# Four residual stages on one core: the node table projected from x itself, three steps behind the attention

## The chip, the core and the metric

The kernel runs on one core of a Trainium2 chip. The metric is device time in microseconds (us), the median of several runs of the whole program; a profiled execution of the same program is taken apart from them. TensorE is called PE in the rows, its weight load PEld, VectorE DVE, ScalarE ACT, GpSimd POOL, SyncE SP.

## What is computed

x holds 128 graphs of 128 nodes with 128 features. Four residual stages follow one another (layer norms in between): a graph attention with a given adjacency (GNN 0), a switch layer that sends each of 16,384 tokens to one of 8 experts (FFN 0), a second graph attention (GNN 1), and a layer whose gate is itself an attention over 524,288 random edges plus one loop per node, with 4 experts of which the top 2 are mixed (FFN 1). The change sits at the joint of the third and the fourth:

```python
x = x + gnn0(layernorm(x), adj, ...)
x = x + ffn0(layernorm(x), ...)
x = x + gnn1(layernorm(x), adj, ...)
x = x + ffn1(layernorm(x), edge_index, ...)

def ffn1(x, ...):
    h = x.reshape(M, 128) @ W_gat
    a_src, a_dst = (h * att_src).sum(-1), (h * att_dst).sum(-1)
    e = leaky_relu(a_src[src] + a_dst[dst])
    alpha = segment_softmax(e, dst)
    agg = segment_sum(h[src] * alpha, dst)
    ...
```

The layer norm of a row is (x - mean) times rstd, rstd = 1 / sqrt(var + eps). Of each node the edges need 24 numbers: 16 columns of h and 4 + 4 attention terms. They form the node table, 16,384 rows of 24.

## The kernel before

The program is two blocks with a barrier between them. **Block 1** (function front) does GNN 0, the routing, the first experts, the sort of the edges' keys and GNN 1, and writes the node table to DRAM. **Block 2** (edges_and_experts1) gathers table rows by edge and runs the last layer.

GNN 1 and all that stands beside it is one software loop over groups of 4 graphs, 32 groups. In step n each engine runs its part of several groups: TensorE turns the probabilities of group n (L221), makes the scores of n+2 (L228, L233, L237), turns the features of n+3 (L245), multiplies probabilities and values of n (L252), and makes the values of n+3 (L264). ACT copies what TensorE turned (L177, L192), makes the leaky branch of the scores (L181), normalises group n+4 (L90) and takes the exponentials of n+2 (L204). DVE divides by the sums and adds to x (L271, L279), takes the maximum of scores and leaky branch and its row maximum (L287, L289), adds the bias to the values of n+3 (L296) and takes the statistics of the finished group (L98). For n up to 16 DVE also adds an expert result to a later group and takes its statistics (combine, L756 and L98); these are called early steps, those from 17 on late ones.

Two more jobs are woven into the same loop. One is the **search**: POOL fetches eight blocks of 64 sorted keys with eight indirect DMAs (L1158) into one of four buffers, DVE compares them with the wanted keys (L818) and counts (L821). There are 32 searches; 25 stand in the loop, in steps n >= 0 whose n mod 4 isn't 3. POOL may begin fetch n only when search n - 4 is counted. The other is the **projection of the node table** (class Projection, tag gat). It follows the attention with a lag of 12 steps: ACT normalises a finished group (L90), TensorE turns it (L378) into bank 1, ACT copies it (L367), TensorE multiplies it with the 24-column weight (L384) into bank 3, and DVE keeps the result in the table in SBUF (L389). The four norms that it needs, of 8 groups each, are made in the loop (L116 to L136, root on ACT at L128). The twelve steps of lag run on behind the loop, with seven searches left beside them or behind them. Where a quarter of the table is kept, SP writes it to DRAM (L905).

In a step each engine follows its program's order, and semaphores say when. Where the projection stands in that order is written out by hand: on TensorE behind L264,

```python
for n in range(-3, GROUPS + LAG):
    att1.pe_step(pe, n, n % 4)
    gat.pe_step(pe, n - LAG, n % 4)
```

and on ACT behind the exponentials, on DVE behind the statistics, the combine and the norms.

Block 2's POOL loop has 31 turns. A turn issues 16 indirect DMAs for one part of the edges (gather(0), L1518), 16 for another (gather(1)), and then two that fetch windows of edge rows for DVE (L1524). Between them POOL takes from SP that the rows gathered before are written to the edge table (rows_out), and from DVE that the window buffer is free (win_free). SP writes the second part of a turn only when DVE has seen the turn's windows (win_seen). DVE scores a window (from L1391 on) and mixes the experts' outputs (L1480). One more pair of windows follows the loop.

Of the kernel before, what the change touches and what calls it, by code (L numbers as in the profile page):

```python
# [14 lines left out]
P = 128  # L15
GRAPHS = NODES = FEAT = 128
PER = 4
# [333 lines left out]


class Projection:
    def __init__(self, sem, tag, x, rstd, shift, ident, weight, cols, into, view, banks, lo=0, turned_in=(0, 1), put_in=(2, 3)):
        self.feat, self.featT = view(lo, 2, PER, FEAT), view(lo + 1024, 2, PER, NODES)
        self.b_featT, self.b_out = ([banks[:, k, :].rearrange("p (v i) -> p v i", v=PER) for k in pair] for pair in (turned_in, put_in))
        self.ahead = len(set(turned_in))
        self.normed, self.turned, self.featT_s, self.projected, self.kept = (
            sem(f"{tag}_{n}") for n in ("normed", "turned", "featT", "projected", "kept"))
        self.x, self.rstd, self.shift, self.ident, self.weight, self.cols, self.into = x, rstd, shift, ident, weight, cols, into  # L360

    def act_step(self, act, n, u):
            a, f = n + 1, n + 2
            if live(a):
                act.wait_ge(self.turned, a + 1)
                ge(act, self.projected, a - 1)
                act.activation(self.featT[:, (u + 1) % 2, :, :], self.b_featT[(u + 1) % 2][:, :, :], ACT.Copy).then_inc(self.featT_s, 1)  # L367
            if live(f):
                ge(act, self.turned, f - 1)
                normalise(act, self.feat[:, u % 2, :, :], self.x, self.rstd, self.shift, f).then_inc(self.normed, 1)  # L370

    def pe_step(self, pe, n, u):
            a = n + 1
            if live(a):
                pe.wait_ge(self.normed, a + 1)
                ge(pe, self.featT_s, a - self.ahead + 1)
                for v in range(PER):
                    last = pe.transpose(self.b_featT[(u + 1) % 2][:, v, :], self.feat[:, (u + 1) % 2, v, :], self.ident)  # L378
                last.then_inc(self.turned, 1)
            if live(n):  # L380
                pe.wait_ge(self.featT_s, n + 1)
                ge(pe, self.kept, n - self.ahead + 1)
                for v in range(PER):
                    last = pe.matmul(self.b_out[u % 2][:, v, 0:self.cols], self.featT[:, u % 2, v, :], self.weight, start=True, stop=True)  # L384
                last.then_inc(self.projected, 1)

    def dve(self, dve, n):
        dve.wait_ge(self.projected, n + 1)
        dve.tensor_scalar(self.into[:, n * PER:(n + 1) * PER, :], self.b_out[n % 2][:, :, 0:self.cols], 1.0, None, ALU.mult).then_inc(self.kept, 1)  # L389


def front(nc, sem, a, x, x_in, stats, scratch, rstd, shift, masked, tab, W, fills, ident, ones, upto, row_id, wanted, counted, found,
# [4 lines left out]
    with ExitStack() as ctx:  # L397
# [74 lines left out]
        gat = Projection(sem, "gat", x, rstd, shift, ident, gat_w[:, :], TAB, tab, view, banks, 4112, (1, 1), (3, 3))  # L472
# [53 lines left out]
        fetched = view(10256, FETCHED, SEARCH, FAN)  # L526
# [30 lines left out]
        def _(dve):  # L557
# [245 lines left out]
            while joined < CHUNK:  # L803
                combine(joined)
                joined += 1
            dve.wait_ge(got_stats, CHUNK)
            gnn1_norms[0].dve_before_root(dve)
            gnn1_norms[0].dve_behind_root(dve)
# [4 lines left out]
            def search():  # L813
                n = searched[0]
                searched[0] += 1
                cols = slice(n * SEARCH, (n + 1) * SEARCH)
                dve.wait_ge(fetched_s[n % FETCHED], 16 * SEARCH * (n // FETCHED + 1))
                dve.tensor_tensor(before[:, :, :], fetched[:, n % FETCHED, :, :],  # L818
                                  wanted[:, cols].unsqueeze(2).to_broadcast([P, SEARCH, FAN]), ALU.is_lt).then_inc(compared, 1)
# [36 lines left out]
            gat_norms[-1].dve_behind_root(dve)  # L856
            for n in range(GROUPS + 1 - LAG, GROUPS):
                gat.dve(dve, n)
                if n % 4 == 3 and searched[0] < SEARCHES // SEARCH:
                    search()  # L860
# [5 lines left out]
        def _(sp):  # L866
# [34 lines left out]
            table_v = table_dram.rearrange("(b i) c -> i b c", i=NODES)  # L901
            for c in range(GROUPS // CHUNK):
                cols = slice(c * CHUNK * PER, (c + 1) * CHUNK * PER)
                sp.wait_ge(gat.kept, (c + 1) * CHUNK)
# [4 lines left out]
        def _(pe):  # L909
# [93 lines left out]
                pe.matmul(to, by[:, :], held_v[:, :, 1], start=False, stop=True).then_inc(summed, 1)  # L1003
            pe.wait_ge(ranked_s, 1)
            pe.wait_ge(gat_made, 2)
            for n in range(-3, GROUPS + LAG):
                att1.pe_step(pe, n, n % 4)
                gat.pe_step(pe, n - LAG, n % 4)

        @block.scalar  # L1010
        def _(act):
# [86 lines left out]
            for n in range(-4, GROUPS + LAG):  # L1098
# [4 lines left out]
                if n > CHUNK and n % CHUNK == 1 and n // CHUNK <= len(gat_norms):  # L1103
                    gat_norms[n // CHUNK - 1].act_root(act)
                    act.wait_ge(gat_norms[n // CHUNK - 1].done, n // CHUNK)
                gat.act_step(act, n - LAG, n % 4)

        @block.gpsimd
        def _(pool):
# [44 lines left out]
            for n in range(SEARCHES // SEARCH):  # L1154
                ge(pool, looked, n - FETCHED + 1)
                for c in range(SEARCH):
                    q = n * SEARCH + c
                    pool.indirect_dma_start(fetched[:, n % FETCHED, c, :], None, keys_dram,  # L1158
                                            bass.IndirectOffsetOnAxis(row_ids[:, q:q + 1], 0)).then_inc(fetched_s[n % FETCHED], 16)


def edges_and_experts1(nc, sem, a, x, rstd, shift, node, found, counted, source_ids, row_id, table_dram, edges_dram, out, ident, ones):
# [8 lines left out]
    with ExitStack() as ctx:  # L1171
# [330 lines left out]
        def _(pool):  # L1502
# [11 lines left out]

            def gather(u):
                take(pool, ids_in[u], 16)
                for c in range(PART_TILES):
# [320 lines left out]
```

## Time and profile before

| | us |
|---|---|
| median of 3 runs | 3116.43 (3116.08 to 3119.05) |
| the profiled execution's own time, its span | 3601.8 |
| TensorE busy | 1935.1 (54%) |
| DVE busy | 2257.8 (63%) |
| ACT busy | 1215.1 (34%) |
| POOL busy | 1857.5 (52%) |

The profiled execution took 485.4 us longer than the median of the runs. It is described by its span alone. The second attention loop lies between about 1284 and 1723 us of that span, block 2's loop between 1881 and 3523.

In a timeline row the columns are: start, duration, engine, line of the program, operation, what it writes and reads, the number of merged instructions, and in brackets the idle time of the engine just before, with what ended it. In a row of groups the two times behind the bar are the busy time and the mean of one in ns, and then the idle time before them, by releaser. In a row of stretches each engine has its busy time with its count of instructions; PEclk is the clock that TensorE was granted, as a part of 2.4 GHz.

### The profile page before, as it was taken

Reading aid. Unit: us, or ns where it says so; the run is one execution under the profiler, and the core shown is the slowest. Engines: PE = TensorE matmul, PEld = TensorE weight load, DVE = VectorE, ACT = ScalarE, POOL = GpSimd, SP = SyncE. Lnnn points to the kernel's source line nnn. Section 1 sums busy time; section 2 is a strip of 40 time slices with the busy share of each in tenths; the row PEclk is TensorE's granted clock in tenths of the full one; section 3 lists DMA queues with packets and bytes.
Section 4 is the critical chain, followed back from the end, with each engine's and each line's share of the span. In section 5 each row is a group of like instructions: output and inputs, shape, how many; then the busy total and the mean of one; then the engine's idle time right before and its main releaser. Section 6 shows DMA issues by size and latency. Waiting matters only on the chain. (4 is left out here: it accounts for less than half of the span.)

```text
span 3601.8 us, 31245 instructions
## 1 busy us (share of the span) xinstructions
PE 1935.1 (54%) x8829; PEld 1316.8 (37%) x8829; DVE 2257.8 (63%) x4422; ACT 1215.1 (34%) x2447; POOL 1857.5 (52%) x1723
## 2 busy tenths in 40 slices
PE   1776642387878645567432455454544444454555
PEld 1555542255655434456311222232222222222223
DVE  8999886989999965554223454454553444544547
ACT  2676754244444323455311122122212122121222
POOL 5400248554544444445575656655655656656561
PEclk9998865699999867777555676676776677767768
DMA  5792001011111121101111111111111111111111
GB/s 198 250 391 84 16 23 39 24 40 37 46 44 41 36 60 40 56 20 23 42 27 23 32 33 32 32 28 38 32 33 32 32 28 31 38 28 32 37 29 30
DMA packets 170130, 192.35 MB, mean 53 GB/s; under 512 B 59241, under 2 KB 126096, under 8 KB 169008
## 3 DMA queue, kind: packets, MB, share of 16 engines
q1 hardware_dynamic: 107616, 118.69, 9.9%
q0 software_dynamic: 57088, 62.48, 8.4%
q10 hardware_dynamic: 5328, 9.97, 0.7%
q8 instruction: 49, 0.80, 0.1%
q14 instruction: 49, 0.40, 0.0%
HBM read 91.70 MB, written 105.25 MB: 55 GB/s over the span
## 5 line engine op out<-in xcount | busy, mean ns | idle before, releaser
L1518 POOL DMA_INDIRECT edge_rows<-node_table,edge_ids x1024 | 1006.5, 983 | 646.2 <-POOLq L1243 345.9
L1646 PE MATMUL x_b_hid<-x_featT,x_w 128*128 128x512 f32 x512 | 362.3, 854 | 281.4 <-PEq L1243 93.5
L1146 POOL DMA_INDIRECT token_results<-arena,token_of x160 | 251.1, 1569 | 294.3 <-ACT arena L1082 216.9
L583 DVE TENSOR_TENSOR sort_ping<-sort_pong 128x1024 f32<-128x1024 f32 (+1 forms) x232 | 395.1, 1744 | 11.3 <-issue 3.8
L1158 POOL DMA_INDIRECT arena<-keys,row_ids x256 | 249.3, 974 | 288.6 <-DVE counts L821 181.0
L583 DVE TENSOR_TENSOR sort_pong<-sort_ping 128x1024 f32<-128x1024 f32 (+1 forms) x230 | 389.9, 1736 | 8.7 <-ACT sort_ping L1016 3.7
L1139 POOL DMA_INDIRECT slots<-arena,send x128 | 177.8, 1389 | 371.9 <-ACT arena L1038 336.9
L1640 PE MATMUL x_b_featT<-ident,x_feat 128*128 128x128 f32 x128 | 34.8, 428 | 581.0 <-issue 385.3
L1653 PEld LDWEIGHTS x_b_res<-x_w,x_hid 128*128 128x128 f32 x2048 | 276.1, 216 | 152.1 <-issue 152.1
L1653 PE MATMUL x_b_res<-x_w,x_hid 128*128 128x128 f32 x2048 | 303.9, 307 | 39.8 <-issue 39.8
L1646 PEld LDWEIGHTS x_b_hid<-x_featT,x_w 128*128 128x128 f32 x512 | 118.9, 262 | 500.2 <-issue 300.9
L1600 ACT ACTIVATE x_hid<-x_b_hid,x_b 128x512 f32<-128x512 f32 x256 | 174.8, 687 | 294.9 <-DMA keys<-sort_pong 129.3
L90 ACT ACTIVATE arena<-x,shift,rstd 128x128 f32<-128x128 f32 x512 | 210.1, 486 | 98.8 <-DMA slots<-arena,send 87.5
L1640 PEld LDWEIGHTS x_b_featT<-ident,x_feat 128*128 128x128 f32 x128 | 22.9, 217 | 587.7 <-issue 587.7
L1607 ACT ACTIVATE w_taken<-w_taken 128x16 f32<-128x16 f32 x32 | 6.9, 216 | 586.5 <-ACTq L1243 357.3
L252 PE MATMUL banks<-arena 128*128 128x129 f32 x512 | 96.4, 347 | 183.3 <-DVE x L279 94.3
L1480 DVE SCALAR_TENSOR_TENSOR x_weighed<-x_b_res,gates,x_weighed 128x128 f32<-128x128 f32 x256 | 72.1, 344 | 193.9 <-DMA adjacent<-in_adj_dram 158.6
L1650 PE MATMUL x_b_res<-x_b,ones 1*128 1x512 f32 x256 | 162.9, 718 | 30.8 <-PEq L1243 27.0
L977 PEld LDWEIGHTS banks<-arena 128*128 128x128 f32 x1280 | 145.9, 192 | 30.3 <-issue 30.3
L252 PEld LDWEIGHTS banks<-arena 128*128 128x128 f32 x512 | 83.9, 248 | 194.1 <-issue 180.0
L977 PE MATMUL banks<-arena 128*128 128x128 f32 x1280 | 153.5, 278 | 0.0
L968 PE MATMUL banks<-arena 128*128 128x512 f32 x320 | 148.5, 608 | 1.8 <-issue 1.8
(346 smaller groups left out, 4059.0 us busy)
## 6 DMA issues: line engine op xcount, KB each, us to landing
edge_table<-zeros SPq DMA_DIRECT2D x8, 5120.0 KB, 35.7
edge_rows<-node_table,edge_ids POOLq DMA_INDIRECT x1024
arena<-slots SPq DMA_DIRECT2D x40, 260.0 KB
slots<-zeros SPq DMA_DIRECT2D x2, 5120.0 KB, 24.4
edge_table<-edge_rows SPq DMA_DIRECT2D x64, 160.0 KB
out_dram<-x_y ACTq DMA_DIRECT2D x33, 256.0 KB
x<-in_x_dram SPq DMA_DIRECT2D x4, 2048.0 KB, 20.2
adjacent<-in_adj_dram SPq DMA_DIRECT2D x32, 256.0 KB, 2.7
```

What stands on the lines that cost most here:

```text
L90: last = act.activation(out[:, u, :], x[:, bass.ds(b, 1), :].rearrange("p o f -> p (o f)"), ACT.Identity, bias=shift[:, bass.ds(b, 1)], sc ...
L252: last = pe.matmul(self.b_near[:, v, 0:FEAT + 1], self.probsT[:, v, :], self.right[:, n % self.deep, v, self.near], start=True, stop=True)
L583: step(dve.tensor_tensor(vb[:, :, t, :], va[:, :, 0, :], va[:, :, 1, :], op))
L977: last = pe.matmul(b_res[:, n % 2, r, :], hid[:, n % 2, c, r * P:(r + 1) * P], w2[:, e % 2, c, :], start=False, stop=(r == PER - 1 and c = ...
L1139: pool.indirect_dma_start(slots_dram, bass.IndirectOffsetOnAxis(send[:, q:q + 1], 0), sent_feat[:, n % 2, v, :], None, bounds_check=EXPERT ...
L1146: pool.indirect_dma_start(rows_dram, bass.IndirectOffsetOnAxis(token_of[:, n % 4, r:r + 1], 0), res[:, n % 2, r, :], None, bounds_check=TO ...
L1158: pool.indirect_dma_start(fetched[:, n % FETCHED, c, :], None, keys_dram, bass.IndirectOffsetOnAxis(row_ids[:, q:q + 1], 0)).then_inc(fetc ...
L1518: pool.indirect_dma_start(rows[:, u, c, :], None, table_dram, bass.IndirectOffsetOnAxis(ids[:, u, c:c + 1], 0)).then_inc(rows_in[u], 16)
L1600: act.activation(hid[:, c, :], b_hid[:, c % 2, :], ACT.Gelu, bias=b1[:, c:c + 1]).then_inc(hid_s, 1)
L1646: pe.matmul(b_hid[:, c % 2, :], w1[:, c // HC1, c % HC1 * P:(c % HC1 + 1) * P], featT[:, :], start=True, stop=True).then_inc(hid_mm, 1)
L1650: pe.matmul(b_res[:, e, :, :], ones[0:1, :], b2[0:1, e, :].unsqueeze(1).to_broadcast([1, UNIT, FEAT]), start=True, stop=False)
L1653: last = pe.matmul(b_res[:, e, v, :], hid[:, e * HC1 + c, v * P:(v + 1) * P], w2[:, e * HC1 + c, :], start=False, stop=(v == UNIT - 1 and ...
```

## The change

It has three parts.

The **projection** no longer normalises. A row of the table is rstd times (x - mean) times W, and the mean can be taken out of the weights: W minus the mean of its column does it, once, before the loop (a matmul with ones into bank 3 and one DVE operation). TensorE turns x itself (L372), ACT only copies (L364), TensorE projects (L378), DVE keeps (L384), with a lag of 3 instead of 12 steps and single buffers in both banks. The rows are scaled with rstd on DVE, a quarter of the table at a time (L389 of the changed program, 128 x 768), in steps 11, 19 and 27 and behind the loop; SP's writes wait for the scaling.

The **searches** have seven fetch buffers instead of four, and stand in steps n >= 1 with n mod 4 not 0 (24 of them); the other eight follow the projection.

**Block 2's loop** issues the windows behind the first eight gathers of the second part, not behind all sixteen.

```diff
 class Projection:
...
     def pe_step(self, pe, n, u):
-            a = n + 1
+            a = n + 2
             if live(a):
-                pe.wait_ge(self.normed, a + 1)
-                ge(pe, self.featT_s, a - self.ahead + 1)
+                pe.wait_ge(self.updated, a + 1)
+                ge(pe, self.featT_s, a)
                 for v in range(PER):
-                    last = pe.transpose(self.b_featT[(u + 1) % 2][:, v, :], self.feat[:, (u + 1) % 2, v, :], self.ident)
+                    last = pe.transpose(self.b_featT[:, v, :], self.x[:, a * PER + v, :], self.ident)
                 last.then_inc(self.turned, 1)
             if live(n):
                 pe.wait_ge(self.featT_s, n + 1)
-                ge(pe, self.kept, n - self.ahead + 1)
+                ge(pe, self.kept, n)
...
-    def act_step(self, act, n, u):
-            a, f = n + 1, n + 2
+    def act_step(self, act, a, u):
             if live(a):
                 act.wait_ge(self.turned, a + 1)
                 ge(act, self.projected, a - 1)
...
-            if live(f):
-                ge(act, self.turned, f - 1)
-                normalise(act, self.feat[:, u % 2, :, :], self.x, self.rstd, self.shift, f).then_inc(self.normed, 1)
...
+    def dve_scale(self, dve, c, chunk, rstd):
+        part, each = self.into[:, c * chunk * PER:(c + 1) * chunk * PER, :], rstd.unsqueeze(2).to_broadcast([P, chunk * PER, self.cols])
+        dve.wait_ge(self.kept, (c + 1) * chunk)
+        dve.tensor_tensor(part, part, each, ALU.mult).then_inc(self.scaled, 1)
...
-        LAG, CHUNK = 12, GROUPS // 4
+        LAG, CHUNK = 3, GROUPS // 4
...
-        BATCH, SEARCH, FETCHED = 8, 8, 4
+        BATCH, SEARCH, FETCHED = 8, 8, 7
...
-                if n >= LAG:
-                    gat.dve(dve, n - LAG)
+                gat.dve_keep(dve, n - LAG - 1)
+                if n > CHUNK and n % CHUNK == LAG:
+                    dve.wait_ge(gat_norms[n // CHUNK - 1].done, n // CHUNK)
+                    gat.dve_scale(dve, n // CHUNK - 1, CHUNK, gat_norms[n // CHUNK - 1].rstd)
...
-                if n >= 0 and n % 4 != 3:
+                if n >= 1 and n % 4:
                     search()
...
+            pe.matmul(b_centre, ones[:, :], gat_w[:, :], start=True, stop=True).then_inc(gat_summed, 1)
+            pe.wait_ge(gat_made, 3)
             for n in range(-3, GROUPS + LAG):
                 att1.pe_step(pe, n, n % 4)
-                gat.pe_step(pe, n - LAG, n % 4)
+                gat.pe_step(pe, n - LAG, (n - LAG) % 4)
...
-                gat.act_step(act, n - LAG, n % 4)
+                gat.act_step(act, n - LAG + 1, (n - LAG + 1) % 4)
...
             with pool.Fori(0, more):
                 gather(0)
                 take(pool, rows_out[1], 16)
-                gather(1)
-
+                take(pool, ids_in[1], 16)
+                gather_columns(1, 0, PART_TILES // 2)
                 take(pool, rows_out[0], 16)
                 take(pool, win_free, 1)
                 windows(win_in)
+                gather_columns(1, PART_TILES // 2, PART_TILES)
```

TensorE in one step of the second attention loop, before; g1 is the attention, gat the projection, arena is SBUF's working space and banks is PSUM:

```order
L252 MATMUL banks<-arena 128x129 [waits g1_updated,g1_right,g1_probsT]
L252 MATMUL banks<-arena 128x129 x3
L264 MATMUL banks<-other,arena 128x128 [waits g1_right,g1_featT]
L264 MATMUL banks<-other,arena 128x128 x3
L378 MATMUL banks<-ident,arena 128x128 [waits gat_featT,gat_normed]
L378 MATMUL banks<-ident,arena 128x128 x3
L384 MATMUL banks<-gat_w,arena 128x24 [waits gat_kept,gat_featT]
L384 MATMUL banks<-gat_w,arena 128x24 x3
L221 MATMUL banks<-ident,arena 128x128 [waits g1_probsT,g1_exped]
L221 MATMUL banks<-ident,arena 128x128 x3
```

The same place with the change:

```order
L252 MATMUL banks<-arena 128x129 [waits g1_updated,g1_right,g1_probsT]
L252 MATMUL banks<-arena 128x129 x3
L264 MATMUL banks<-other,arena 128x128 [waits g1_right,g1_featT]
L264 MATMUL banks<-other,arena 128x128 x3
L372 MATMUL banks<-ident,x 128x128 [waits gat_featT,g1_updated]
L372 MATMUL banks<-ident,x 128x128 x3
L378 MATMUL banks<-gat_w,arena 128x24 [waits gat_kept,gat_featT]
L378 MATMUL banks<-gat_w,arena 128x24 x3
L221 MATMUL banks<-ident,arena 128x128 [waits g1_probsT,g1_exped]
L221 MATMUL banks<-ident,arena 128x128 x3
```

The transposes stand at the same place and now read x as soon as the attention has updated it. In step n they turn group n - 1 where they turned n - 11, and the wait on gat_featT is for ACT's copy of group n - 2 (before, of n - 12). ACT makes that copy in its own step n, where it made the copy of n - 11 in step n before and TensorE needed the one of step n - 1.

POOL in block 2's loop, before:

```order
L1532 UNCONDITIONAL_BRANCH
L1518 DMA edge_rows<-node_table,edge_ids 128x20 x32
L1524 DMA win<-edge_table,win_ids 128x800 x2
L1532 REGISTER_ALU
L1532 COMPARE_AND_BRANCH
```

With the change:

```order
L1546 UNCONDITIONAL_BRANCH
L1532 DMA edge_rows<-node_table,edge_ids 128x20 x24
L1538 DMA win<-edge_table,win_ids 128x800 x2
L1532 DMA edge_rows<-node_table,edge_ids 128x20 x8
L1546 REGISTER_ALU
L1546 COMPARE_AND_BRANCH
```

The two window DMAs moved ahead of the last eight gathers of a turn, and with them POOL's waits for rows_out[0] and for win_free.

## Rows read from the trace of the kernel before

**Rows 1.** The page's first line, the span of the profiled execution.

```profile
span 3601.8 us, 31245 instructions
```

**Rows 2.** POOL in block 2's loop: groups (busy us, mean ns, idle before), then timeline.

```profile
L1518 POOL DMA_INDIRECT edge_rows<-node_table,edge_ids x960 | 941.1, 980 | 625.0 <-POOLq L1243 343.6 <-issue 281.4
L1524 POOL DMA_INDIRECT win<-edge_table,win_ids x60 | 57.2, 953 | 18.3 <-issue 18.3
...
2537.18 1.00 POOL L1524 DMA_INDIRECT win<-edge_table,win_ids  x1 [0.30 <-issue]
...
2569.81 1.22 POOL L1518 DMA_INDIRECT edge_rows<-node_table,edge_ids  x1 [10.37 <-POOLq L1243]
```

**Rows 3.** Timeline of DVE in block 2: the last window's first and last work.

```profile
3567.88 0.89 DVE L1391 TENSOR_TENSOR win_score<-win,masked 128x320 f32<-128x320 f32 x2 [1.23 <-DVEq L1243]
...
3598.05 1.12 DVE L1480 SCALAR_TENSOR_TENSOR x_y<-x_b_res,gates,x_weighed 128x128 f32<-128x128 f32 x4 [0.18 <-DVEq L1243]
```

**Rows 4.** Timeline of the second attention loop: one late step, all engines.

```profile
1641.68 0.59 ACT L181 ACTIVATE arena<-banks 128x512 f32<-128x512 f32 x1
1641.83 1.16 PE L252 MATMUL banks<-arena 128*128 128x129 f32 x8 [0.22 <-ACT arena L177]
...
1643.80 0.60 PE L378 MATMUL banks<-ident,arena 128*128 128x128 f32 x4
1644.01 0.69 DVE L296 TENSOR_TENSOR arena<-banks,bias 128x512 f32<-128x512 f32 x1 [0.29 <-PE banks L264]
...
1644.24 0.97 PE L384 MATMUL banks<-gat_w,arena 128*128 128x24 f32 x8
...
1645.34 0.59 ACT L367 ACTIVATE arena<-banks 128x512 f32<-128x512 f32 x1
...
1645.51 0.22 DVE L116 TENSOR_TENSOR scratch<-stats 128x32 f32<-128x32 f32 x1
...
1646.55 0.25 DVE L389 TENSOR_SCALAR masked<-banks 128x96 f32<-128x96 f32 x1
...
1647.49 0.60 PE L245 MATMUL banks<-ident,arena 128*128 128x128 f32 x4
1647.83 0.59 ACT L181 ACTIVATE arena<-banks 128x512 f32<-128x512 f32 x1
...
1649.65 0.80 PE L252 MATMUL banks<-arena 128*128 128x129 f32 x5 [1.56 <-DVE x L279]
```

**Rows 5.** Timeline of the same loop, one early step with combine and search.

```profile
1479.90 2.06 PE L252 MATMUL banks<-arena 128*128 128x129 f32 x8 [3.56 <-issue]
...
1483.49 0.69 DVE L296 TENSOR_TENSOR arena<-banks,bias 128x512 f32<-128x512 f32 x1 [2.42 <-PE banks L264]
...
1486.37 0.24 DVE L389 TENSOR_SCALAR masked<-banks 128x96 f32<-128x96 f32 x1
...
1489.46 1.64 PE L252 MATMUL banks<-arena 128*128 128x129 f32 x8 [1.89 <-DVE x L279]
```

**Rows 6.** Timeline of TensorE in the first attention loop, two idle stretches.

```profile
196.31 2.06 PE L252 MATMUL banks<-arena 128*128 128x129 f32 x8 [2.24 <-DVE arena L275]
...
271.60 1.13 PE L252 MATMUL banks<-arena 128*128 128x129 f32 x8 [2.09 <-DVE arena L275]
```

**Rows 7.** Timeline of the tail behind the second attention loop.

```profile
1722.78 2.06 PE L252 MATMUL banks<-arena 128*128 128x129 f32 x8 [13.05 <-DVE x L279]
...
1775.12 1.28 POOL L1158 DMA_INDIRECT arena<-keys,row_ids  x1 [3.42 <-DVE counts L821]
...
1787.08 0.69 DVE L818 TENSOR_TENSOR adjacent<-arena,wanted 128x512 f32<-128x512 f32 x1 [7.89 <-DMA arena<-keys,row_ids]
```

**Rows 8.** Stretch of the tail: PE, PEld, DVE, ACT, POOL busy; PEclk, DMA share.

```profile
1724.00:1768.00 44.00, 30.92 (x139) 28.85 (x139) 10.35 (x34) 24.94 (x57) 25.57 (x27) 0.50 0.18 30
```

**Rows 9.** Timeline of DVE in the tail, the last group's end and the last norm's.

```profile
1727.43 0.17 DVE L271 RECIPROCAL att_small<-banks 128x4 f32<-128x4 f32 x1
...
1734.89 0.19 DVE L136 SCALAR_TENSOR_TENSOR shift<-scratch,rstd 128x32 f32<-128x32 f32 x1
```

More of the change, by code:

```diff
@@ L353, with __init__ @@
 class Projection:
[L354 to L360, printed above, removed]
-    def act_step(self, act, n, u):
-            a, f = n + 1, n + 2
+    def __init__(self, sem, tag, x, updated, ident, weight, cols, into, featT, b_featT, b_out):
+        self.turned, self.featT_s, self.projected, self.kept, self.scaled = (
+            sem(f"{tag}_{n}") for n in ("turned", "featT", "projected", "kept", "scaled"))
+        self.x, self.updated, self.ident, self.weight, self.cols, self.into = x, updated, ident, weight, cols, into
+        self.featT, self.b_featT, self.b_out = featT, b_featT, b_out
+    def act_step(self, act, a, u):
             if live(a):
@@ L366, in act_step @@
                 ge(act, self.projected, a - 1)
-                act.activation(self.featT[:, (u + 1) % 2, :, :], self.b_featT[(u + 1) % 2][:, :, :], ACT.Copy).then_inc(self.featT_s, 1)
-            if live(f):
-                ge(act, self.turned, f - 1)
-                normalise(act, self.feat[:, u % 2, :, :], self.x, self.rstd, self.shift, f).then_inc(self.normed, 1)
+                act.activation(self.featT[:, u % 2, :, :], self.b_featT[:, :, :], ACT.Copy).then_inc(self.featT_s, 1)
     def pe_step(self, pe, n, u):
-            a = n + 1
+            a = n + 2
             if live(a):
-                pe.wait_ge(self.normed, a + 1)
-                ge(pe, self.featT_s, a - self.ahead + 1)
+                pe.wait_ge(self.updated, a + 1)
+                ge(pe, self.featT_s, a)
                 for v in range(PER):
-                    last = pe.transpose(self.b_featT[(u + 1) % 2][:, v, :], self.feat[:, (u + 1) % 2, v, :], self.ident)
+                    last = pe.transpose(self.b_featT[:, v, :], self.x[:, a * PER + v, :], self.ident)
                 last.then_inc(self.turned, 1)
@@ L381, in pe_step, with dve_keep @@
                 pe.wait_ge(self.featT_s, n + 1)
-                ge(pe, self.kept, n - self.ahead + 1)
+                ge(pe, self.kept, n)
                 for v in range(PER):
-                    last = pe.matmul(self.b_out[u % 2][:, v, 0:self.cols], self.featT[:, u % 2, v, :], self.weight, start=True, stop=True)
+                    last = pe.matmul(self.b_out[:, v, 0:self.cols], self.featT[:, u % 2, v, :], self.weight, start=True, stop=True)
                 last.then_inc(self.projected, 1)
-    def dve(self, dve, n):
-        dve.wait_ge(self.projected, n + 1)
-        dve.tensor_scalar(self.into[:, n * PER:(n + 1) * PER, :], self.b_out[n % 2][:, :, 0:self.cols], 1.0, None, ALU.mult).then_inc(self.kept, 1)
+    def dve_keep(self, dve, n):
+        if live(n):
+            dve.wait_ge(self.projected, n + 1)
+            dve.tensor_scalar(self.into[:, n * PER:(n + 1) * PER, :], self.b_out[:, :, 0:self.cols], 1.0, None, ALU.mult).then_inc(self.kept, 1)
+    def dve_scale(self, dve, c, chunk, rstd):
+        part, each = self.into[:, c * chunk * PER:(c + 1) * chunk * PER, :], rstd.unsqueeze(2).to_broadcast([P, chunk * PER, self.cols])
+        dve.wait_ge(self.kept, (c + 1) * chunk)
+        dve.tensor_tensor(part, part, each, ALU.mult).then_inc(self.scaled, 1)
 def front(nc, sem, a, x, x_in, stats, scratch, rstd, shift, masked, tab, W, fills, ident, ones, upto, row_id, wanted, counted, found,
@@ L468, in front @@
             "step", "less", "exp", "chosen", "ranked", "placed", "order", "done"))
-        LAG, CHUNK = 12, GROUPS // 4
-        gat = Projection(sem, "gat", x, rstd, shift, ident, gat_w[:, :], TAB, tab, view, banks, 4112, (1, 1), (3, 3))
+        LAG, CHUNK = 3, GROUPS // 4
+        b_centre = banks[:, 3, 0:TAB]
+        gat_summed = sem("gat_summed")
+        gat = Projection(sem, "gat", x, att1.updated, ident, gat_w[:, :], TAB, tab, view(4112, 2, PER, NODES),
+                         banks[:, 1, :].rearrange("p (v i) -> p v i", v=PER), banks[:, 3, :].rearrange("p (v i) -> p v i", v=PER))
         gat_norms = []
@@ L525, in front @@
         flat_adj = adjacent[:, :, :].rearrange("p c f -> p (c f)").bitcast(F32)
-        fetched = view(10256, FETCHED, SEARCH, FAN)
+        in_arena = view(10256, 4, SEARCH, FAN)
+        in_masks = flat_adj[:, SEARCH * FAN:4 * SEARCH * FAN].rearrange("p (u c f) -> p u c f", u=3, c=SEARCH)
+        fetched = [in_arena[:, u, :, :] for u in range(4)] + [in_masks[:, u, :, :] for u in range(3)]
         before = flat_adj[:, 0:SEARCH * FAN].rearrange("p (c f) -> p c f", c=SEARCH)
@@ L805, in _ @@
                 joined += 1
+            dve.wait_ge(gat_summed, 1)
+            dve.scalar_tensor_tensor(gat_w[:, :], b_centre, -1.0 / FEAT, gat_w[:, :], ALU.mult, ALU.add).then_inc(gat_made, 1)
             dve.wait_ge(got_stats, CHUNK)
@@ L817, in search @@
                 dve.wait_ge(fetched_s[n % FETCHED], 16 * SEARCH * (n // FETCHED + 1))
-                dve.tensor_tensor(before[:, :, :], fetched[:, n % FETCHED, :, :],
+                dve.tensor_tensor(before[:, :, :], fetched[n % FETCHED],
                                   wanted[:, cols].unsqueeze(2).to_broadcast([P, SEARCH, FAN]), ALU.is_lt).then_inc(compared, 1)
@@ L853, in _ @@
                     link(dve.tensor_reduce(counted, tiles[:, :], AX_X, ALU.add))
-                if n >= 0 and n % 4 != 3:
+                if n >= 1 and n % 4:
                     search()
             gat_norms[-1].dve_behind_root(dve)
[L857 to L860, printed above, removed]
+            for n in range(GROUPS - LAG, GROUPS):
+                gat.dve_keep(dve, n)
+            dve.wait_ge(gat_norms[-1].done, GROUPS // CHUNK)
+            gat.dve_scale(dve, GROUPS // CHUNK - 1, CHUNK, gat_norms[-1].rstd)
             while searched[0] < SEARCHES // SEARCH:
@@ L1516, in gather, with gather_columns @@
                 take(pool, ids_in[u], 16)
-                for c in range(PART_TILES):
+                gather_columns(u, 0, PART_TILES)
+            def gather_columns(u, first_column, end_column):
+                for c in range(first_column, end_column):
                     pool.indirect_dma_start(rows[:, u, c, :], None, table_dram,
```

4 lines of the change are left out of this document (2 added, 2 removed).

## Prediction

> **What bounds the kernel now.** I read the page, the POOL's groups in block 2's loop, that loop's last turn, then block 1 step by step. The median of the runs is 3116.43 us; the profiled execution spans 3601.8 us [rows 1], 485.4 more, so a total of the trace can't be carried over as it is; single stretches without stalls can. In 30 turns of block 2's loop (54.7 us each) POOL spends (941.1 + 57.2)/30 = 33.3 us on indirect DMAs and (281.4 + 18.3)/30 = 10.0 us between them, 43.3 in all, and 343.6/30 = 11.5 waiting [rows 2]. The wait stands between the loop's two gathers: windows issued at 2537.18, second gather not before 2569.81 [rows 2], because its buffer's write waits until DVE has begun this window. [...] The runs lack 485.4 us, of which this wait can explain 343.6; so I take the runs' loop as **bound by POOL's issuing**, 43.3 us a turn, and the other 141.8 us as stalls in block 1. A fifth of a per cent, 6.2 us, is what a measurement can tell from no change.
>
> In block 1 the second attention loop matters. A late step (no token combine) lasts 1641.83 to 1649.65 = 7.82 us, with 1.04 us of quarter norm on DVE (1645.51 to 1646.55): 6.78; ACT works without a gap and needs 6.15 (1641.68 to 1647.83) [rows 4]. Three steps of four hold a search: about 6.6 on average. An early step (with combine) lasts 1479.90 to 1489.46 = 9.56 with a search, part of it on a slow TensorE [rows 5]; a search is two DVE operations of 0.69 [rows 7], so 9.2 on average, and about 7.8 where TensorE stays at full clock. Behind the loop comes a tail, in which the projection of eleven groups runs alone: last L252 at 1722.78, last fetch issued at 1775.12, its compare at 1787.08 [rows 7].
>
> **The change, part by part.** The sum is made against the runs' median through stretches that show no stall; the profiled span of 3601.8 would shrink by more (below).
>
> *Tail.* With a lag of 3 instead of 12, eleven groups leave the tail. Before: 1787.08 - 1722.78 = 64.3, of which some 2.6 look like stall: 61.7. After: PV 2.1, held to norm at most 7.65 (1727.43 to 1734.89 + 0.19, with a search of 1.4 in between that now comes later) [rows 9], so 6.2; then the last copy 0.6, its projection and keep 2.3, the scaling 1.05 (768 columns at L296's 0.69 for 512 [rows 4]), a search 1.4, and the last fetch as before 1787.08 - 1775.12 = 12.0: 25.6 to 26. Gain about **35**. The seven other searches hide under that fetch. In the profile the tail runs at a granted clock of 0.50, the lower of the two levels (1.2 GHz), with TensorE busy for 30.92 of 44 us [rows 8]. If the runs hold 2.4 GHz there, up to half of that goes, 15 us, and the gain is 20. Since TensorE idles for a third of this stretch whatever came before it, I take the row's, 35, and keep 20 for the range.
>
> *Late steps.* The new order couples the engines. TensorE's transposes of group n-1 now stand in step n and wait for ACT's copy of group n-2 (one bank), which ACT does in the same step behind its exponentials; those wait for DVE's maximum, which waits for this step's scores. So TensorE cannot begin step n+1 before ACT has ended step n. The ring: copy from L181's start to L367's end 1641.68 to 1645.93 = 4.25; then transposes, projection, probabilities and scores up to L245, 1643.80 to 1647.49 = 3.69, and 0.16 to the scores' end; three hand-offs of about 0.1 [rows 4]: **8.4 us** at full clock against 6.6. The four removed normalisations (1.65) come off ACT, which no longer sets the pace. TensorE now idles some 2 us in each step. What follows such idles: of 13 idle stretches of 1.7 to 2.3 us in the two attention loops, 196.31 to 1489.46, six are followed by matmuls at about half speed (2.06 us for L252's eight) and seven by full speed (1.13) [rows 6]. Slow matmuls cost about 1.6 in a step: 0.93 for L252, and somewhat less for the shorter groups behind it. So 8.4 + 6/13 x 1.6 = 9.1: 2.5 more, for 15 late steps **+37**. Ends: 1.8 (always full) and 3.4 (always slow).
>
> *Early steps.* Here a second ring is longer: TensorE's projection of n-3 waits for DVE's keep of n-4 in the same step, which stands behind bias, statistics and combine. L252 to L296 2.18 (1641.83 to 1644.01); L296 to the end of keep 3.12 (1483.49 to 1486.61); projection to L245 3.25 (1644.24 to 1647.49); to the next L252 0.6; 0.1 [rows 4, 5]: 9.25 at full clock against 7.8, or 10.7 against 9.2 at the slow one. +1.45 either way, 14 steps: **+21**.
>
> *Norms and scaling.* Three quarter norms (1.04 DVE, root and its table on ACT) now stand before the copy that the ring needs: 1.3 each, **+4**. Three scalings of 1.05 hide on DVE beside the ring's idle time; if they don't, +3. Centring the weights, a matmul and a small DVE operation before the loop: 0.3.
>
> *Searches.* One fewer in the loop, three more buffers; POOL is ahead of them already, 0.
>
> *Windows earlier.* POOL issues them 8 x 1.273 = 10.2 us sooner [rows 2]. The turn's issuing stays 43.3, so the period does, but the last window, the late one and the end come that much sooner: **-10**. Each turn now has 8 issues instead of 16 between the first gather's end and the wait for its write: 10.2 us against 20.4. The write's issue and landing are not seen to take as long anywhere in the trace: 0.
>
> Sum: -35 + 37 + 21 + 4 - 10 = +17, or **3134 us**.
>
> **Rivals.** (1) *TensorE stays at full clock.* Late 1.8 x 15 = 27; early the idles become shorter than today's 3.56 and 1.89 [rows 5], so 9.25 stands against 9.2, 0; +4 - 45: -14, **3102**. For: seven of thirteen idles; against: the three in this loop all slowed. This one ends on the other side; it decides as soon as over half of the idles cost nothing.
> (2) *The wait in POOL's loop isn't all gone in the runs.* Then earlier windows let DVE begin sooner and free the second gather, every turn. At a tenth of 11.5 us a turn, 34 us less: **3100**. For: 343.6 is much [rows 2]; against: the 485.4 are already needed.
> (3) *The clock falls in every step.* 3.4 x 15 = 51 + 21 + 4 - 45 = +31: **3148**. For: the idle at 1489.46 [rows 5]. The Trainium skill, TensorE: Matmul & The Clock Gate, section on a second failure mode (depth-cycling of the PSUM queue), says that small idles between groups of matmuls let the clock swing between its two levels and that throughput is lost in the re-warming. By that rule the change would land here rather than at 3102; the trace agrees in six cases of thirteen.
> (4) *The end isn't earlier*, since the last window waits for something else: +27, **3144**.
> (5) *POOL waits for the first gather's write* every turn; with 2 us over the 10.2, 31 turns: +62, **3196**.
>
> **Numbers.** Forecast 0.38, rivals 0.24, 0.12, 0.12, 0.08, 0.06. The forecast's own range is 3119 to 3149: 15 us for the tail (20 instead of 35) on one side, as much for hand-offs and slow steps on both. Faster by over 6.2 us: most of (1) (0.18), half of (2) (0.07), a little of the forecast (0.03): 0.28. Within: 0.06 of (1), 0.05 of (2), 0.06 of the forecast, 0.01 of (4): 0.18. Slower: 0.29 + 0.12 + 0.07 + 0.06 = 0.54. The range 3090 to 3162 leaves out (5), the low part of (2) and the edges of (1) and (3), under 0.2.
>
> **What would show it.** Right: in late steps an ACT copy of the projection ends just before TensorE's transposes begin, with the step at 8.4 to 10 us; the tail from the last L252 to the last compare near 26 us; in POOL's loop much of the 343.6 gone, because windows come earlier against the wait, so that the profiled span shrinks by far more than the runs. Wrong: late steps under 7.5 us; POOL waiting between the first eight issues of the second gather and the windows; a tail still over 40 us; runs shorter by over 40 us, which would mean that the loop's wait is real in the runs.

## The result, and the profile after

The changed kernel takes 3166.19 us against 3116.55: 1.0162 times as long (95% interval 1.0150 to 1.0174), 50 us slower. The forecast was 3134 with a range up to 3162: the side was right, the size a third of what came.

The profile that the prediction read was stretched by 485 us. A second profile of the same kernel (the first experiment) spans 3115.3 us, as the runs do, and is the one that the changed kernel's span of 3167.5 is compared with here. Cut at six places that both traces have, the difference lies thus:

| stretch | before | changed | difference | forecast |
|---|---|---|---|---|
| start to L252 of step 0 | 1321.13 | 1323.30 | +2.2 | 0.3 |
| L252 of step 0 to L252 of step 31 | 265.55 | 350.78 | **+85.2** | +62 |
| to the last search's compare | 65.62 | 34.64 | **-31.0** | -35 |
| to block 2's first gather | 8.65 | 12.61 | +4.0 | 0 |
| to the first window | 85.25 | 75.27 | -10.0 | -10 |
| 30 turns of the loop | 1297.66 | 1299.29 | +1.6 | 0 |
| last window of the loop to the end | 71.44 | 71.61 | +0.2 | 0 |

So 23 of the 33 us that the forecast lacks lie in the second attention loop. The +2.2 of the start are spread: the windows alone (below), whose first block is that of before, reach that place at 1322.95, the kernels built on the changed one between 1319.91 and 1322.77. A row per kernel shows that loop by engines (busy us of PE, PEld, DVE, ACT and POOL with counts; then TensorE's granted clock as a part of 2.4 GHz, DMA share, GB/s). Before, in the second profile:

```profile
1321.00:1587.00 266.00, 191.96 (x1271) 169.66 (x1270) 203.09 (x581) 181.49 (x440) 174.34 (x178) 0.87 0.19 51
```

The changed kernel:

```profile
1323.00:1674.00 351.00, 250.34 (x1384) 209.91 (x1382) 209.27 (x594) 155.38 (x366) 195.74 (x204) 0.79 0.16 43
```

DVE has 6 us more to do and ACT 26 us less, in a loop that is 85 us longer: neither is what fills it. TensorE is busy 58 us longer with 113 more records, and its granted clock falls from 0.87 to 0.79. Its row in a late step, before (the answer to [rows 4], step 21):

```profile
1519.33 1.13 PE L252 MATMUL banks<-arena 128*128 128x129 f32 x8 [0.39 <-DVE x L279]
...
1522.44 0.64 PE L221 MATMUL banks<-ident,arena 128*128 128x128 f32 x4
...
1523.13 1.02 PE L233 MATMUL banks<-arena,key_row 128*128 128x512 f32 x2
...
1525.86 1.13 PE L252 MATMUL banks<-arena 128*128 128x129 f32 x8 [0.39 <-DVE x L279]
```

and a late step of the changed kernel, step 23, TensorE with ACT's copy (L364) ahead of it:

```profile
1596.70 1.06 PE L252 MATMUL banks<-arena 128*128 128x129 f32 x8
...
1600.14 0.58 ACT L364 ACTIVATE arena<-banks 128x512 f32<-128x512 f32 x1
...
1600.87 0.63 PE L372 MATMUL banks<-ident,x 128*128 128x128 f32 x4 [2.11 <-ACT arena L364]
...
1602.15 1.05 PE L221 MATMUL banks<-ident,arena 128*128 128x128 f32 x4
...
1603.42 1.91 PE L233 MATMUL banks<-arena,key_row 128*128 128x512 f32 x2
1605.12 1.30 PE L237 MATMUL banks<-query_row,arena 128*128 128x128 f32 x8
...
1606.70 1.06 PE L252 MATMUL banks<-arena 128*128 128x129 f32 x8
```

6.53 us have become 10.00. TensorE waits 2.11 us for ACT's copy of the same step. L372 right behind the wait runs at full speed, but from L221 on, 1.3 us behind its end, matmuls run at about half speed: L221 takes 1.05 where it took 0.64, L233 1.91 where it took 1.02. An early step (step 7) has a second wait, for DVE's keep:

```profile
1394.48 1.06 PE L252 MATMUL banks<-arena 128*128 128x129 f32 x8
...
1398.65 0.63 PE L372 MATMUL banks<-ident,x 128*128 128x128 f32 x4 [2.11 <-ACT arena L364]
1399.85 1.04 PE L378 MATMUL banks<-gat_w,arena 128*128 128x24 f32 x8 [0.57 <-DVE masked L384]
...
1401.98 1.91 PE L233 MATMUL banks<-arena,key_row 128*128 128x512 f32 x2
...
1405.28 1.06 PE L252 MATMUL banks<-arena 128*128 128x129 f32 x8
```

And where norms are made, the roots on ACT (L128, with a table load of 1.28) stand before the copy, and TensorE waits for all of it; step 17, 14.30 us:

```profile
1534.68 1.28 ACT L128 ACT_TABLE_LOAD   x1
...
1536.90 0.23 ACT L128 ACTIVATE scratch<-scratch 128x32 f32<-128x32 f32 x1 [0.69 <-DVE shift L136]
...
1537.82 0.60 ACT L364 ACTIVATE arena<-banks 128x512 f32<-128x512 f32 x1 [0.69 <-DVE shift L136]
...
1538.56 1.09 PE L372 MATMUL banks<-ident,x 128*128 128x128 f32 x4 [5.37 <-ACT arena L364]
```

The tail shrank as the table says, though DVE waits for the last two fetches of the searches in it (answers to [rows 7]; the last row is DVE's first work in block 2):

```profile
1674.08 2.09 PE L252 MATMUL banks<-arena 128*128 128x129 f32 x8 [0.69 <-ACT arena L177]
...
1698.76 0.71 DVE L825 TENSOR_TENSOR adjacent<-arena,wanted 128x512 f32<-128x512 f32 x1 [2.91 <-DMA arena<-keys,row_ids]
...
1708.72 0.69 DVE L825 TENSOR_TENSOR adjacent<-arena,wanted 128x512 f32<-128x512 f32 x1 [8.54 <-DMA arena<-keys,row_ids]
...
1718.52 0.09 DVE L1268 MEMSET due<- 128x32 f32 x1 [7.92 <-PEq L1699]
```

In block 2 the wait of 343.6 us that [rows 2] shows for POOL is gone, but so it is in the second profile of the kernel before. Before:

```profile
L1518 POOL DMA_INDIRECT edge_rows<-node_table,edge_ids x1024 | 995.8, 972 | 313.2 <-issue 289.2 <-POOLq L1243 24.0
```

The changed kernel:

```profile
L1532 POOL DMA_INDIRECT edge_rows<-node_table,edge_ids x1024 | 997.8, 974 | 313.4 <-issue 295.8 <-POOLq L1254 17.6
```

### The profile page after: what moved, and what is told of

Its sections match the earlier page's. It is cut to its first block and busy times, and to the rows that moved or that the text cites. A ratio compares the mean times of both kernels' runs of the same rounds, so it can differ in the third digit from the quotient of the medians.

```text
span 3167.5 us, 31131 instructions
## 1 busy us (share of the span) xinstructions
PE 1827.4 (58%) x8831; PEld 1254.0 (40%) x8831; DVE 2258.7 (71%) x4427; ACT 1156.4 (37%) x2319; POOL 1847.7 (58%) x1723
## 5 line engine op out<-in xcount | busy, mean ns | idle before, releaser
L1402 DVE TENSOR_TENSOR win_score<-win,masked 128x320 f32<-128x320 f32 x64 | 28.7, 489 | 447.3 <-DMA win<-edge_table,win_ids 446.1
L1661 PE MATMUL x_b_hid<-x_featT,x_w 128*128 128x512 f32 x512 | 311.6, 763 | 28.3 <-PEq L1254 28.3
L1668 PEld LDWEIGHTS x_b_res<-x_w,x_hid 128*128 128x128 f32 x2048 | 246.0, 197 | 97.4 <-issue 97.4
L1668 PE MATMUL x_b_res<-x_w,x_hid 128*128 128x128 f32 x2048 | 271.0, 287 | 0.0
L1169 POOL DMA_INDIRECT arena<-keys,row_ids x160 | 156.8, 980 | 135.3 <-DVE counts L828 52.4
L1661 PEld LDWEIGHTS x_b_hid<-x_featT,x_w 128*128 128x128 f32 x512 | 107.7, 239 | 218.5 <-ACT x_hid L1615 126.4
L90 ACT ACTIVATE arena<-x,shift,rstd 128x128 f32<-128x128 f32 x384 | 157.7, 486 | 96.9 <-DMA slots<-arena,send 85.5
L1665 PE MATMUL x_b_res<-x_b,ones 1*128 1x512 f32 x256 | 143.7, 641 | 27.8 <-PEq L1254 27.8
L986 PEld LDWEIGHTS banks<-arena 128*128 128x128 f32 x1280 | 145.9, 192 | 30.3 <-issue 30.3
L1428 DVE TENSOR_TENSOR win_msg<-win,win_score 128x1280 f32<-128x1280 f32 x64 | 92.7, 1490 | 77.9 <-DVEq L1254 77.9
```

What stands on the lines that cost most here:

```text
L90: last = act.activation(out[:, u, :], x[:, bass.ds(b, 1), :].rearrange("p o f -> p (o f)"), ACT.Identity, bias=shift[:, bass.ds(b, 1)], sc ...
L986: last = pe.matmul(b_res[:, n % 2, r, :], hid[:, n % 2, c, r * P:(r + 1) * P], w2[:, e % 2, c, :], start=False, stop=(r == PER - 1 and c = ...
L1169: pool.indirect_dma_start(fetched[n % FETCHED][:, c, :], None, keys_dram, bass.IndirectOffsetOnAxis(row_ids[:, q:q + 1], 0)).then_inc(fetc ...
L1661: pe.matmul(b_hid[:, c % 2, :], w1[:, c // HC1, c % HC1 * P:(c % HC1 + 1) * P], featT[:, :], start=True, stop=True).then_inc(hid_mm, 1)
L1665: pe.matmul(b_res[:, e, :, :], ones[0:1, :], b2[0:1, e, :].unsqueeze(1).to_broadcast([1, UNIT, FEAT]), start=True, stop=False)
L1668: last = pe.matmul(b_res[:, e, v, :], hid[:, e * HC1 + c, v * P:(v + 1) * P], w2[:, e * HC1 + c, :], start=False, stop=(v == UNIT - 1 and ...
```

## The experiments

**The kernel before, profiled again.** No edit.

> The kernel before, unchanged, profiled once more, to have its stages in an execution that is not stretched. Theory (POOL's issuing sets block 2's loop): windows 43 us apart and under 50 us of waiting for POOL in the loop's gathers in all; attention steps near 9 us early and 6.6 late; the first gather of block 2 near 1660 us. Rival (the wait of 11.5 us a turn is real): windows over 47 us apart, 100 us or more of waiting left, and block 1 shorter by as much.

3117.5 us, a span of 3115.3. Windows are 43.3 us apart (1746.20 to 3043.86 in 30 turns), POOL's gathers wait 24.0 us in all, the first gather starts at 1660.95, late steps without norms take 6.4 us and early ones 8.2. POOL's issuing sets block 2's loop; the long waits of [rows 2] are those of that one execution. What stretched it was not found.

**The windows alone**, in the kernel before:

```diff
-                gather(1)
-
+                take(pool, ids_in[1], 16)
+                gather_columns(1, 0, PART_TILES // 2)
                 take(pool, rows_out[0], 16)
                 take(pool, win_free, 1)
                 windows(win_in)
+                gather_columns(1, PART_TILES // 2, PART_TILES)
```

> The kernel before with the third part of the change alone: windows issued behind the first eight gathers of the second part. Theory: the period stays at 43 us and only the end comes sooner, 10 us less than before, about 3106. Rival (the loop's wait is real and goes): 34 us less or more. Rival (the first gather's write is waited for each turn): no gain or slower.

3108.32 us, 0.9971 of before (0.9960 to 0.9983): 8 us less, and POOL's waiting for rows and windows together falls from 42.3 to 29.6 us, not by hundreds. This part does what the prediction said, and no more.

**ACT's copy first**, in the changed kernel:

```diff
+                gat.act_step(act, n - LAG + 1, (n - LAG + 1) % 4)
                 att1.act_step(act, n, n % 4)
...
                     act.wait_ge(gat_norms[n // CHUNK - 1].done, n // CHUNK)
-                gat.act_step(act, n - LAG + 1, (n - LAG + 1) % 4)
```

> The changed kernel with one thing moved: ACT makes the projection's copy at the head of its step, not behind the exponentials, so TensorE's transposes no longer wait for the same step's exponentials. Theory (the ring TensorE, DVE maximum, exponentials, copy, TensorE sets the step): late steps fall from 10 to 14 us to 7 or 8, TensorE stays at its upper clock in most of them, and the time falls by 35 to 60 us, to 3105 to 3130. Rival (the loop is longer because eleven groups' work moved into it, or because DVE is full): under 10 us change, near 3160.

3143.36 us (1.0085 of before, 1.0068 to 1.0101): 23 us less than changed, less than the theory's lower end. The wait for the copy is gone, and in its place TensorE waits longer for the keep, which stands behind the whole of DVE's step:

```profile
1382.65 0.60 PE L372 MATMUL banks<-ident,x 128*128 128x128 f32 x4
...
1385.73 0.24 DVE L384 TENSOR_SCALAR masked<-banks 128x96 f32<-128x96 f32 x1
...
1386.12 1.23 PE L378 MATMUL banks<-gat_w,arena 128*128 128x24 f32 x8 [2.87 <-DVE masked L384]
```

2.11 + 0.57 before the edit, 2.87 after it: the early step shown stays at 10.80 us. Late steps fall to 7.6 and 9.3, in turn.

**Keep first as well:**

```diff
                 att1.dve_held(dve, n - 1)
+                gat.dve_keep(dve, n - LAG - 1)
...
-                gat.dve_keep(dve, n - LAG - 1)
```

> The same, and DVE's keep of the projection right behind the division by the sums, not behind bias, statistics, combine and norms. Theory: the second ring (projection waits for a keep behind DVE's whole step) holds the early steps at 9 to 11 us and goes with this: another 10 to 25 us less than with the copy alone, 3085 to 3115. Rival (DVE itself is full in early steps): within 6 us of the copy alone.

3083.58 us, 0.9898 of before (0.9881 to 0.9914): 60 us less than with the copy alone, and 33 less than before the change. It is below the theory's range. TensorE no longer waits in the projection, and the loop takes 256.3 us, 9 less than before the change though it holds the eleven groups of the old tail:

```profile
1369.11 1.13 PE L252 MATMUL banks<-arena 128*128 128x129 f32 x8 [1.73 <-DVE x L279]
...
1372.90 1.02 PE L233 MATMUL banks<-arena,key_row 128*128 128x512 f32 x2
...
1376.97 1.13 PE L252 MATMUL banks<-arena 128*128 128x129 f32 x8 [1.72 <-DVE x L279]
```

```profile
1321.00:1577.00 256.00, 197.04 (x1378) 175.75 (x1376) 206.41 (x592) 155.00 (x366) 192.42 (x195) 0.89 0.22 57
```

The same matmuls keep TensorE busy for 197 us at a granted clock of 0.89 where the changed kernel needs 250 at 0.79. That the loop was full of work, the rival, is out.

**Keep first alone** (the second diff without the first):

> The changed kernel with DVE's keep moved to the front of its step, ACT's copy left behind the exponentials. Theory (two rings side by side, each near 8.3 to 9.3 us at full clock): alone it brings little, 0 to 35 us, since the copy's ring takes over; early steps fall to those of the late ones, 8.3 to 10 us; 3130 to 3166. Rival (the keep's ring is the whole loss): 3083 to 3095, as with both moved.

3135.64 us (1.0077, 1.0058 to 1.0097): 31 less than changed. Copy 23, keep 31, both 83: each ring hides the other, and as long as one stands the clock keeps falling behind its wait (late steps still 8.3 or 10.0).

**TensorE kept busy in the wait**, in the changed kernel:

```diff
+                for _ in range(8 if 2 <= a < GROUPS - 2 else 0):
+                    pe.matmul(self.spare, self.ident, self.ident, start=True, stop=True)
                 pe.wait_ge(self.updated, a + 1)
                 ge(pe, self.featT_s, a)
```

Nothing is left out; the added products are not read.

> The changed kernel, with eight more matmuls on TensorE in each step, into a free bank, where it waits for ACT's copy (their result is not read). The waits stay, TensorE just isn't idle in them. Theory (over half of the loop's loss is the clock that falls behind those waits): the matmuls of a step run at their full-clock durations, late steps go from 10.0 to 8.3 to 8.7 us, and the time falls by 25 to 50 us, to 3115 to 3140. Rival (the waits alone cost the time, the slow matmuls lie in their shadow): within 6 us of the changed kernel, or slower by the added work.

3127.96 us (1.0047, 1.0030 to 1.0063): 38 less than changed, by adding 28 x 1.95 = 55 us of matmuls. The wait for the copy still ends when it did, but the matmuls behind it are quick:

```profile
1557.71 1.06 PE L252 MATMUL banks<-arena 128*128 128x129 f32 x8
1559.61 1.95 PE L370 MATMUL banks<-ident 128*128 128x128 f32 x16
1561.88 0.63 PE L374 MATMUL banks<-ident,x 128*128 128x128 f32 x4 [0.32 <-ACT arena L364]
1563.84 1.02 PE L233 MATMUL banks<-arena,key_row 128*128 128x512 f32 x2
1566.03 1.06 PE L252 MATMUL banks<-arena 128*128 128x129 f32 x8
```

```profile
1322.00:1633.00 311.00, 251.28 (x1792) 226.85 (x1817) 207.25 (x590) 154.14 (x363) 197.48 (x203) 0.92 0.18 48
```

8.32 us a step instead of 10.00, and the granted clock is 0.92. The loop takes 313.1 us where the changed kernel's takes 350.8. So of the 85 us that the loop lost some 38 are the clock behind the waits; the other 47 are the waits themselves and what slow matmuls are left in the norm steps, which this run doesn't part.

**The copy before the roots**, behind the exponentials:

```diff
                 att1.act_step(act, n, n % 4)
+                gat.act_step(act, n - LAG + 1, (n - LAG + 1) % 4)
                 if n in ROOTED_AT:
```

> The changed kernel with ACT's copy of the projection between the exponentials and the norms' roots, so that only the roots leave the ring. In steps 9, 17 and 25 TensorE waited 5.37, 5.37 and 4.46 us for the copy instead of 2.11. Theory: 9 us of waiting go, and some of the slow matmuls behind them: 8 to 16 us less than the changed kernel, 3150 to 3158. Rival (the root's time only moves to the next step, where ACT is late with the probabilities): under 4 us.

3161.57 us (1.0153, 1.0136 to 1.0170), 5 less than changed by the medians, with the kernel before beside it 2 less as well: the intervals of the two ratios overlap, so a gain isn't shown, and the theory's range is missed. In steps 9 and 17 TensorE's wait of 5.37 becomes 2.11 for the copy and 2.66 for the keep, since DVE stands in the same chain of norms. Moving the copy alone does not take the loss out of the norm steps.

**Four fetch buffers and the old search slots**, in the kernel with both moved:

```diff
-        BATCH, SEARCH, FETCHED = 8, 8, 7
+        BATCH, SEARCH, FETCHED = 8, 8, 4
...
-                if n >= 1 and n % 4:
+                if n >= 0 and n % 4 != 3:
```

> The kernel with both moved (copy and keep first), with the second part of the change undone: four fetch buffers and the old slots of the searches. Theory: in the quick loop POOL's 256 fetches at 1.25 us are what ends block 1 last, and with four buffers POOL waits behind the norm steps: 0 to 12 us slower than with both moved, 3083 to 3096. Rival (the buffers don't matter): within 3 us.

3103.71 us (0.9963, 0.9951 to 0.9975): 20 slower than with seven, more than expected. The loop is as quick (260.0), but POOL waits 36.8 us for counted searches, where it waited 4.8, and the last compare ends 25 us later. In the quick loop the 256 fetches are the end of block 1, so the second part of the change (buffers and slots together) is worth 20 us there.

**Windows behind four gathers**, with both moved:

```diff
-                gather_columns(1, 0, PART_TILES // 2)
+                gather_columns(1, 0, PART_TILES // 4)
...
-                gather_columns(1, PART_TILES // 2, PART_TILES)
+                gather_columns(1, PART_TILES // 4, PART_TILES)
```

> The kernel with both moved, with block 2's windows issued behind four gathers of the second part instead of eight. In the changed kernel the first part's last gather was issued at 2133.12 and its write went out at 2136.19 and takes 2.1, which four issues (5.0) just cover. Theory: 4 to 5 us sooner, near 3079. Rival (POOL now waits for the write each turn): slower, 1 us a turn would be 31 us.

3079.32 us, 0.9889 of before (0.9872 to 0.9905). By the medians that is 4 less than with eight, but the kernel before beside it is 2 less as well and the intervals overlap: the runs don't tell the two apart. In the traces the first window comes 4.1 us sooner behind the first gather (70.31 us for 74.41), and from that gather to the end it is 2.6 us less. By its median it is the quickest kernel of the study, 36 us below before (3114.86 beside it) and 87 below the changed one.

**The same with five buffers** (FETCHED 5):

> The quickest kernel so far (copy and keep first, windows behind four gathers) with five fetch buffers instead of seven. With seven buffers the passage from block 1 to block 2 takes 8.0 us between DVE's last work and its next, with four 4.2. Theory (the passage grows with the semaphores that are freed there; five buffers are enough, since with seven POOL waited 4.8 us in all and with four 36.8): the passage falls by 1 to 3 us and POOL waits 5 to 25 us: 3072 to 3095. Rival (the passage has nothing to do with the buffers): 8.0 us as before.

3097.19 us (0.9955, 0.9938 to 0.9971): 18 slower than with seven, and 2 above the theory's range. POOL waits 26.9 us for counted searches. The passage between the blocks is shorter, 5.36 us for 8.27.

## Why the prediction was right and wrong

**Right.** What bounds block 2's loop, read from a stretched profile, held to the first decimal (43.3 us a turn), and with it the gain of 10 us and the absence of any other. Both rings are there, with the members and almost the lengths named: 8.3 us measured at full clock in late steps (8.29 and 8.32) for 8.4 forecast, and 9.1 in early ones (with the wait filled) for 9.25. The tail gave 31 us of 35; it fell short since POOL still had three fetches of 10 us to issue behind the last L252 (the first at 1676.06, with no wait between them), where the sum had room for one.

**Wrong: "8.4 + 6/13 x 1.6 = 9.1".** This is the step that failed, in late steps mildly and in early ones fully. I took from thirteen idle stretches that fewer than half of the waits are followed by slow matmuls, and I judged each by the group right behind it. That group doesn't tell: in the changed kernel 17 steps have a wait of 2.1 us for the copy, L372 right behind it takes 0.63, its full speed, in all 17, and L233 later in the step is slow in 15. The trace that I read had such a case, a wait that looks harmless by the group behind it, L252 at its full 1.13, and then L261 at 2.08 for the 1.12 of an earlier step:

```profile
273.57 1.12 PE L261 MATMUL banks<-arena,bilinear 128*128 128x512 f32 x2 [0.41 <-ACT arena L192]
...
365.80 1.13 PE L252 MATMUL banks<-arena 128*128 128x129 f32 x8 [2.26 <-DVE arena L275]
...
367.77 2.08 PE L261 MATMUL banks<-arena,bilinear 128*128 128x512 f32 x2
```

(Between the two times that the prediction names, that trace has 15 such stretches, not 13: six with slow matmuls right behind them, and two more, at 290.45 and 365.80, with slow ones 1 to 2 us later.) In all, L233 is slow in 25 of the changed kernel's 27 steps from 2 to 28 (1.64 to 1.92 us for 1.02), against 2 of 29 before. A late step became 9.4 on average, 3.0 more than its 6.4, where I had 2.5. For early steps I let the clock be the same on both sides ("+1.45 either way"): it wasn't, since the steps before the change run L221 to L245 at full speed even where L252 and L264 are slow, and the new waits stand just ahead of those. Eight plain early steps (3 to 7, 11 to 13) went from 8.2 to 11.15, +3.0 instead of +1.45; that most of them hold a projection now that had none before costs nothing, as the same steps of the kernel with both moved show, 8.2 on average. The Trainium skill, TensorE: Matmul & The Clock Gate, in the section on its second failure mode, says that small idles between groups of matmuls make the clock swing and cost throughput. The trace agrees with it: 0.79 granted against 0.89 for the same work without the waits, and 38 us back when the waits were filled. As a rival I had given it a chance of 0.12.

**Wrong: "1.3 each, +4" for the norms.** Ten steps around the norms (8 to 10, 15 to 18, 24 to 26) went from 9.0 to 13.35 us on average, 44 us in all; their plain rings account for 20 of the forecast, the norms for 4, so 20 were missing. I counted three chains of one norm. There are two norms in steps 9 and 17, DVE's ten small operations stand ahead of the keep, and ACT's two roots and the table loads ahead of the copy, so that TensorE waits 2.9 us for the keep in one step, beside 2.1 for the copy, and 5.4 for the copy in the next, and L233 is slow in both.

In figures, the loop's miss of 23 us is 20 for the norm steps, 12 for plain early steps and 3 for plain late ones, less 12 that the first, the special and the last steps (0 to 2, 14, 29 to 31) did better than I had them. The other misses are +4 of the tail, +4 of the passage between the blocks and +2 each at the start and in the loop of block 2: 50 - 17 = 33, with 2 between spans and medians. (3116.43 + 17 is 3133, not 3134; the times of rivals 2 to 5 are high in the same way.)

**"Searches: 0"** was an answer to a question that the forecast loop doesn't put: with steps of 10 us POOL is ahead. With both rings gone it decides 20 us.

**Rivals.** (1) falls with the count of slow steps. (2) is shown wrong by the second profile and by the windows alone. (3) named the clock and was still too short, at 3148: its loop is 76 us longer, where 85 were measured, since like the forecast it has 4 us for the norms and no clock in early steps. (4) and (5) fall: the end came 10 us sooner and no wait for the write appeared.

## What to carry to other kernels

When a stage is woven closer behind another, ask on each engine whether it now waits for something that the other engine does at the end of the same step: a copy or a keep at the tail of an in-order step closes a ring over all engines, and moving it to the head of the step (two lines here) turned 50 us of loss into 33 us of gain. Undo such rings all at once before judging one, since each hides the others. A wait of 2.11 us on TensorE made a late step here 1.8 us longer by itself (8.32 with the wait filled, 6.53 before) and, where slow matmuls followed, another 1.7 (10.00); whether it does so can be tried by filling the wait. To see from a trace what a wait does to the clock, look at all matmuls up to the next wait, not only at the first group behind it.

## What had not been expected of the hardware

The passage between the two blocks, where semaphores are freed and all engines meet, depends on how many fetch buffers there are, each with a semaphore of its own. DVE's first work in block 2 comes after an idle time of 4.17 us with four buffers, 5.36 with five, 8.00 with seven:

```profile
1654.34 0.09 DVE L1268 MEMSET due<- 128x32 f32 x1 [4.17 <-PEq L1699]
```

```profile
1650.77 0.09 DVE L1268 MEMSET due<- 128x32 f32 x1 [5.36 <-PEq L1699]
```

```profile
1633.10 0.09 DVE L1268 MEMSET due<- 128x32 f32 x1 [8.00 <-PEq L1699]
```

That is about 1.3 us for each buffer, and the 4.0 of the table. The other traces agree: 4.01 and 4.05 in the two kernels with the first block of before (four buffers), 7.77 to 8.27 in the others with seven. Which of the buffer's semaphore or its instructions makes it was not tried apart; a further semaphore as such costs far less, since the kernel with both moved and four buffers has one more than the kernel before (gat_summed) and needs 4.17 for 4.01.

The slow matmuls don't stand right behind a wait of 2.1 us: in the late step above L372 and L378 run at 0.63 and 0.97, their full speed, and L221 1.3 us behind the wait's end is the first slow one. And a wait of 1.7 us before L252 in early steps of the kernel with both moved (the two rows shown there) is followed by none (granted clock 1.00 from 1354 to 1394), where 2.11 in the steps of the changed kernel, with 0.57 more in early ones, is followed by slow matmuls nearly always. What tells the two apart was not settled.
